# Layer 0 of a two-layer fp32 kernel: the front's bank in a new order, delta's replicas behind its store, 1+e on GpSimd

## The chip, the cores and the metric

The program runs on one core of a Trainium2 chip, in one launch. The metric is the device time of the whole program in microseconds. The engines are PE (TensorE), DVE (VectorE), ACT (ScalarE), POOL (GpSimd) and SP (SyncE, which issues nearly all DMAs here). Each engine works through its own list of instructions in order and waits on semaphores; nothing is reordered while it runs.

## What is computed

Two layers, each a sequence mixer and an expert layer added to the residual. The change touches layer 0 alone, on 8192 tokens of width 128:

```
xn    = layernorm(x)
u, z  = split(rmsnorm(xn) @ in_proj)            # 256 + 256 channels
xi    = silu(conv4(u) + conv_b)
dt, B, C = split(xi @ x_proj)                   # 8, 16, 16
delta = softplus(dt @ dt_w + dt_b)
h     = exp(delta * A) * h + (delta * xi) * B   # a scan over time, 16 states a channel
y     = (sum over states of h * C + xi * D) * silu(z)
p     = softmax(xn @ Wr + br); gate = p where the sorted cumulative sum < 0.8, else 0
ffn   = sum over 8 experts of gate_e * (relu(xn @ W1_e + b1_e) @ W2_e + b2_e)
x     = x + (xn + y @ out_proj) + ffn
```

## The kernel before

Layer 0 goes through the tokens in 16 iterations of 512 tokens. In an iteration the scan has 32 tiles of 128 x 512 (two halves of the channels, four groups of states, four channel blocks), and each of the 8 experts has four `up` products into two banks (`UP`) and a `down` product into `DN`.

The order of the work is written out by hand. An iteration is 32 half-slots h = 0..31, and every engine runs through the same h in its own list:

- DVE: `scan(h)`, then `times_c(h)` (the product with C). The scan needs `dA` (h) and `dBx`.
- ACT: `make_da(h + 2)`, exp(delta * A), into a ring of three PSUM banks; for h mod 4 = 0 and 1 also two `relu`, one before and one after it; for h mod 4 = 3 the gate times the expert's output.
- POOL: at even h `make_dbx`, the products delta * x * B for half-slots h + 2 and h + 3; at h mod 4 = 2 one `accumulate`.
- PE: `up` products at h mod 4 = 0 and 1, the sum over states (`add_states`, bank `YS`) at h mod 4 = 1, one half of a `down` product at 2 and at 3. An `up` of one group of four half-slots is used by the `down` of the next group.

Between these, each engine makes the *front* of the next iteration: norm, transposes, in_proj, convolution, x_proj, delta, logits, gate and silu(z). The front's TensorE products share one PSUM bank, `FRO`, so they follow each other as the bank is emptied. The tables `PE_AT`, `ACT_AT`, `DVE_AT`, `POOL_AT` and `SP_AT` give for each piece the half-slot after whose own work it is put into the engine's list; a negative number counts back from the end of the iteration before. Pieces of one engine with the same h stand in the order of the code of `fore`.

Softplus is made as max(v,0) + log(1+e) with e = exp(-|v|), v = dt @ dt_w + dt_b, and with a correction of what is lost in 1+e: `one_w` = 1+e; `soft` = (one_w - 1) - e (DVE); `umax` = umax - soft ("r", POOL); ln(1+e) (ACT, which loads another table for it and the first again after it); `lnw`, that logarithm where 1+e is over 1 (DVE); delta = umax + lnw (POOL); dx = delta * xi (POOL). The gate's first steps are the logits, their maximum (DVE "lg"), the difference (POOL "lg"), and the exponential (ACT "gexp").

delta, dx, B and C go to HBM and come back as replicas over the partitions (`REP`: 1 MB for each of delta and dx and each half, `BC`: 1 MB for each two groups of states). SP issues these stores and loads, in its own order.

Of the kernel before, what the change touches and what calls it, by code (L numbers as in the profile page):

```python
# [51 lines left out]
def layer0(nc, ctx, t, dram, scratch):  # L52
# [35 lines left out]
    forget = sb("forget", [P, T0 // L]); mean = sb("mean", [P, NT]); rstd = sb("rstd", [P, NT]); rrms = sb("rrms", [P, NT])  # L88
# [26 lines left out]
    front = signal("front", 11)  # L115
# [4 lines left out]
    sp_done = signal("sp_done", 3); relu_done = signal("relu_done", E0 * FB); da_ready = signal("da_ready", TILES); gated = signal("gated", E0)  # L120
# [134 lines left out]
    def _(sp):  # L255
# [68 lines left out]
        def fore(h, n, q):  # L324
# [47 lines left out]
    def _(pe):  # L372
        for s in (front, upf, downf, sumf, outf):
            pe.sem_inc(s.sem, 2 * s.per)
# [71 lines left out]
        def slot(h, it, par, first=False, final=False, last_front=False):  # L446
# [13 lines left out]
            if h == PE_AT["out"] and not first:  # L460
                if final:
                    output(it - 1, 1 - par, lambda: pe.wait_ge(gT_copied.sem, gT_copied.at(it, 1)))
                else:
                    output(it - 1, 1 - par, lambda: pe.wait_ge(conv_step.sem, conv_step.at(it + 1, 6)))

        def fore(h, n, q):
            if h == PE_AT["xqt"]:
# [46 lines left out]
            for k in range(HALF):  # L514
                if h == PE_AT[f"z{k}"]:

                    if k == 0:
                        pe.wait_ge(gate_step.sem, gate_step.at(n, 1))
                    elif bank(n, k) is FRO:
                        pe.wait_ge(z_done.sem, z_done.at(n, 1))  # L520
                    nc.tensor.matmul(bank(n, k)[:], inproj[:, (2 + k) * P:(3 + k) * P], xrT[:], start=True, stop=True).then_inc(front.sem, 1)
            if h == PE_AT["gt"]:

                pe.wait_ge(gate_made.sem, gate_made.at(n, 5))
                pe.wait_ge(z_done.sem, z_done.at(n, 2))
                nc.tensor.transpose(FRO[0:J0 * E0, 0:P], gate[:, q].rearrange("p j e -> p (j e)"), ident[:]).then_inc(front.sem, 1)
# [13 lines left out]
    def _(act):  # L540
# [103 lines left out]
        def fore(h, n, q):  # L644
# [50 lines left out]
            for k in range(HALF):  # L695
                if h == ACT_AT[f"tz{k}"]:

                    if k == 0:
                        act.wait_ge(delta_done.sem, delta_done.at(n, 1))
# [1206 lines left out]
```

## Time and profile before

| what | value |
|---|---|
| median of three runs | 2101.07 us (2100.62 to 2101.74) |
| the profiled execution | 2100.98 us, its span 2099.2 us |
| around the span | 1.78 us |
| PE busy | 1894.3 us, 90% |
| DVE busy | 1675.4 us, 80% |
| ACT busy | 1341.5 us, 64% |
| POOL busy | 1309.0 us, 62% |
| first scan of layer 0 / last statistics of layer 0 | 74.3 us / 1426.8 us |

The span is the time from the first to the last instruction of the profiled execution; its own time is longer by what lies around the span. Busy is the time in which an engine ran an instruction. Layer 0's sixteen iterations lie between the first scan and the last statistics; the rest belongs to the start and to layer 1.

### The profile page before, as it was taken

The numbers are of one execution on the slowest core, as the hardware profiler recorded it, in microseconds if no ns is written. First come the engines' busy times: TensorE is split into PE (matmuls) and PEld (weight loads), VectorE is DVE, ScalarE is ACT, GpSimd is POOL, SyncE is SP. The second block draws the span as 40 slices with busy tenths as digits, with TensorE's granted clock in tenths as the row PEclk, the third lists the DMA queues.
The fourth block names the chain that finished last, engine by engine and source line by source line (L and its number), as shares of the span: only waits on it lengthen the run. The fifth ranks groups of instructions, "written<-read, shape, count | busy, mean of one in ns | idle before, by whom it ended". The sixth has DMA issues, their size and how long they took to land. (4 is left out here: it accounts for less than half of the span.)

```text
span 2099.2 us, 39052 instructions
## 1 busy us (share of the span) xinstructions
PE 1894.3 (90%) x14321; PEld 1106.2 (53%) x14321; DVE 1675.4 (80%) x2731; ACT 1341.5 (64%) x2423; POOL 1309.0 (62%) x1005
## 2 busy tenths in 40 slices
PE   5789999999999999999999999994799999998985
PEld 3445555555555555555555555552455555554552
DVE  5588888898898987988979888883888888886655
ACT  3577776776777767777677677761355555554652
POOL 2577877868878777787786887863343333333650
PEclk7899999999999999999999999996799999999997
DMA  8633615426245163362451633605444444455558
GB/s 202 155 85 73 141 40 125 101 52 141 75 90 133 30 140 87 67 141 58 106 120 43 136 87 68 141 6 156 123 119 123 117 117 117 117 137 154 163 145 245
DMA packets 211994, 234.86 MB, mean 112 GB/s; under 512 B 31718, under 2 KB 150414, under 8 KB 207694
## 3 DMA queue, kind: packets, MB, share of 16 engines
q1 hardware_dynamic: 207116, 227.95, 43.7%
q0 software_dynamic: 2048, 4.18, 0.7%
q8 instruction: 115, 1.88, 0.4%
q14 instruction: 75, 0.61, 0.1%
q10 hardware_dynamic: 2640, 0.24, 0.1%
HBM read 165.48 MB, written 66.85 MB: 111 GB/s over the span
## 5 line engine op out<-in xcount | busy, mean ns | idle before, releaser
L731 POOL TENSOR_TENSOR dBx<-REP,BC 128x1024 f32<-128x1024 f32 x256 | 603.6, 2360 | 254.7 <-DVE dA L904 224.6
L904 DVE TENSOR_TENSOR_SCAN dA<-dA,dBx 128x512 f32<-128x512 f32 x512 | 626.3, 1223 | 154.4 <-POOL dBx L731 109.9
L403 PE MATMUL UP<-xnT,W 128*128 128x512 f32 x1024 | 517.6, 623 | 49.3 <-ACT hT L605 44.6
L412 PEld LDWEIGHTS DN<-W,hT 128*128 128x128 f32 x4096 | 469.5, 192 | 98.0 <-issue 66.9
L412 PE MATMUL DN<-W,hT 128*128 128x128 f32 x4096 | 495.1, 278 | 0.3 <-ACT GD L612 0.3
L596 ACT ACTIVATE dA<-REP,A 128x512 f32<-128x512 f32 x512 | 354.0, 695 | 86.5 <-DVE PR L913 78.0
L605 ACT ACTIVATE hT<-UP,b 128x512 f32<-128x512 f32 x512 | 355.6, 695 | 66.1 <-PE UP L403 60.6
L913 DVE TENSOR_TENSOR PR<-dA,BC 128x512 f32<-128x512 f32 x512 | 353.6, 691 | 16.0
L403 PEld LDWEIGHTS UP<-xnT,W 128*128 128x128 f32 x1024 | 179.1, 194 | 286.9 <-issue 163.7
L1808 DVE TENSOR_REDUCE NM<-S 128x4 f32<-128x1024 f32 (+1 forms) x192 | 234.1, 1219 | 76.0 <-PE S L1353 75.8
L1567 ACT ACTIVATE PT<-S 128x1024 f32<-128x1024 f32 x192 | 197.1, 1027 | 94.8 <-PE S L1353 94.0
L612 ACT ACTIVATE GD<-DN,gate 128x128 f32<-128x128 f32 x512 | 145.6, 366 | 126.6 <-PE DN L412 126.1
L741 POOL TENSOR_TENSOR FF<-FF,GD 128x512 f32<-128x512 f32 x128 | 162.8, 1272 | 6.1 <-ACT GD L612 6.1
L424 PE MATMUL YS<-PR,fold 128*32 128x512 f32 x1024 | 139.7, 618 | 0.5 <-DVE PR L913 0.5
L1621 POOL TENSOR_TENSOR t<-t 128x512 f32<-128x512 f32 x32 | 40.7, 1271 | 133.4 <-DVE t L1732 133.3
L1409 PE MATMUL OT<-PT,V 128*9 128x256 f32 x1024 | 84.7, 392 | 7.2 <-ACT PT L1567 5.2
L1548 ACT CAST CS<-ACC 128x256 bf16<-128x256 f32 x64 | 23.8, 373 | 84.9 <-PE ACC L1465 83.7
L1627 POOL TENSOR_TENSOR SPL<-t,SPL 128x512 bf16<-128x512 f32 x32 | 37.2, 1162 | 65.6 <-ACT SPL L1573 65.6
L970 DVE SCALAR_TENSOR_TENSOR xch<-FRO,convw,xch 128x510 f32<-128x510 f32 (+2 forms) x93 | 69.2, 744 | 8.6 <-ACT xch L655 6.4
L1561 ACT COPY OSB<-OT 128x512 f32<-128x512 f32 x64 | 37.5, 586 | 59.2 <-PE OT L1411 59.2
L424 PEld LDWEIGHTS YS<-PR,fold 128*32 128x32 f32 x1024 | 20.4, 109 | 102.8 <-issue 68.1
L797 POOL TENSOR_TENSOR xch<-xch,soft 128x1024 f32<-128x1024 f32 x16 | 37.6, 2350 | 43.3 <-DVE soft L979 43.3
(251 smaller groups left out, 2618.1 us busy)
## 6 DMA issues: line engine op xcount, KB each, us to landing
BC<-s_b SPq DMA_DIRECT2D x128, 256.0 KB, 5.9
REP<-s_dx SPq DMA_DIRECT2D x124, 256.0 KB, 7.5
REP<-s_delta SPq DMA_DIRECT2D x124, 256.0 KB, 8.9
s_parts<-SPL SPq DMA_DIRECT2D x64, 192.0 KB
KS<-s_parts SPq DMA_DIRECT2D x64, 192.0 KB
QS<-s_parts SPq DMA_DIRECT2D x64, 192.0 KB
s_dx<-tz SPq DMA_DIRECT2D x16, 512.0 KB, 3.1
s_y<-zeros SPq DMA_DIRECT2D x32, 256.0 KB, 2.9
```

Of the source, the lines that this page charges most:

```text
L403: nc.tensor.matmul(UP[k % 2][:], W1[:, e % E0, f * P:(f + 1) * P], xnT[:, q, :], start=True, stop=True).then_inc(upf.sem, 1)
L412: last = nc.tensor.matmul(DN[:, j * P:(j + 1) * P], hT[:, e % 2, f, j * P:(j + 1) * P], W2[:, e, f, :], start=(f == 0), stop=(f == FB - 1))
L424: last = nc.tensor.matmul(YS[CB * j:CB * j + CB, :], fold[:], PR[:, (DB * b + j) % (2 * DB), :], start=(q == 0), stop=(q == NQ - 1), tile_ ...
L596: nc.scalar.activation(dA[:, k % 3, :], DR[:, h, j, :], ACT.Exp, scale=A[:, h, j, q:q + 1]).then_inc(da_ready.sem, 1)
L605: nc.scalar.activation(hT[:, e % 2, f, :], UP[k % 2][:], ACT.Relu, bias=b1[:, e % E0, f:f + 1]).then_inc(relu_done.sem, 1)
L612: last = nc.scalar.activation(GD[:, e % 2, j, :], DN[:, j * P:(j + 1) * P], ACT.Copy, scale=gate[:, par, j, e:e + 1])
L731: nc.gpsimd.tensor_tensor(dBx[:, s % 2], DX[:, h, j:j + 2, :], BC[:, q // 2, q % 2, :].unsqueeze(1).to_broadcast([P, 2, T0]), ALU.mult).th ...
L741: nc.gpsimd.tensor_tensor(FF[:, par], FF[:, par], GD[:, e % 2], ALU.add).then_inc(acc_done.sem, 1)
L904: nc.vector.tensor_tensor_scan(h, h, dBx[:, k // 2 % 2, k % 2, :], 0.0, ALU.mult, ALU.add).then_inc(scan_done.sem, 1)
L913: nc.vector.tensor_tensor(PR[:, k % (2 * DB), :], dA[:, k % 3, :], BC[:, q // 2, 2 + q % 2, :], ALU.mult).then_inc(prod_done.sem, 1)
L1567: nc.scalar.activation(PT[:, u // 3, u % 3, :], S2[:].rearrange("p b w -> p (b w)"), ACT.Exp, scale=SCALE).then_inc(exp_done.sem, 1)
L1808: nc.vector.tensor_reduce(NM[:, 0 if a == 0 else 1, :].rearrange("p (r i) -> p r i", r=2)[:, :, heads], S1[:].rearrange("p r (j k) -> p r ...
```

## The change

Four things are changed, all in layer 0.

1. The front's bank goes in another order. The first transpose (`xqt`) moves from h = -2 to -6, the two products of u (`x0`, `x1`) and their convolutions four half-slots earlier, `xnt` from 17 to 4, x_proj from 10 to 8, `dt0` and `dt1` from 12 and 16 to 10 and 14, `z1` now stands ahead of `z0` (20 and 23, were 27 and 23), and the transpose of the gate goes from the front into the next iteration (h = 16). POOL's norm of the tokens (`xm`, `xq`, `xs`) moves from -7, -4, -4 to -19, -17, -15, and `EARLY` from 7 to 19 so that this can be written.
2. `one_w` = 1+e is an addition on POOL (h = 15) in place of an ACT instruction (h = 17), with a tile `unit` of ones broadcast as second operand; the correction is written to `one_w` and not over `soft`, and the test for a lost e reads e itself. ACT's exp goes from 17 to 14.
3. On POOL `r` goes from 20 to 18 and `dx` from 23 to 21, where it stands ahead of `lg`.
4. On SP the loads of delta's first replicas follow its store directly, and those of dx stand behind the loads of B and C.

```diff
-    umax, lnw, one_w, tanhz = xch, th, tz, xch
+    umax, lnw, one_w = xch, th, tz
...
-    EARLY = 7
-    PE_AT = dict(xqt=-2, x0=0, x1=4, out=8, xproj=10, dt0=12, dt1=16, xnt=17, logits=19, z0=23, z1=27, gt=29)
-    ACT_AT = dict(xr=-2, tap0=2, tap1=4, tanh=6, dtb=10, d0=14, d1=16, xn=18, exp=17, one=17, ln=18, gexp=20, tz0=23, tz1=27, gt=29)
-    DVE_AT = dict(conv0=3, conv1=5, xi=8, soft=19, lg=19, lnw=20, gate1=23, z0=25, gate2=27, z1=29, ev1=3, store=9, stat=12, ev0=21)
-    POOL_AT = dict(xm=-7, xq=-4, xs=-4, ff=10, r=20, dx=23, rank=23, yz1=3, yz0=22, delta=20, lg=21, keep=27)
+    EARLY = 19
+    PE_AT = dict(xqt=-6, x0=-4, x1=0, xnt=4, out=6, xproj=8, dt0=10, dt1=14, gt=16, logits=18, z1=20, z0=23)
+    ACT_AT = dict(xr=-6, tap0=-2, tap1=0, tanh=2, xn=5, dtb=9, d0=10, d1=14, exp=14, gt=17, ln=18, gexp=20, tz1=21, tz0=25)
+    DVE_AT = dict(conv0=-1, conv1=1, xi=4, soft=17, lg=19, lnw=20, gate1=23, z1=23, z0=25, gate2=27, ev1=3, store=7, stat=11, ev0=21)
+    POOL_AT = dict(xm=-19, xq=-17, xs=-15, ff=9, one=15, r=18, dx=21, rank=23, yz1=3, yz0=22, delta=20, lg=21, keep=27)
...
-    SP_AT = dict(bst=11, dst=15, est=23, bc0=26, save=10, load=12)
+    SP_AT = dict(bst=9, dst=15, est=23, bc0=26, save=8, load=10)
...
+                if not start:
+                    load_delta(0, n, q)
             elif h == SP_AT["est"]:
...
-                else:
-                    load_delta(0, n, q)
-                    load_dx(0, n, q)
             elif h == SP_AT["bc0"] and not start:
                 load_states(0, n, q)
+                load_dx(0, n, q)
...
+            if h == PE_AT["z1"]:
+
+                pe.wait_ge(gate_step.sem, gate_step.at(n, 1))
+                nc.tensor.matmul(bank(n, 1)[:], inproj[:, 3 * P:4 * P], xrT[:], start=True, stop=True).then_inc(front.sem, 1)
+            if h == PE_AT["z0"]:
+
+                if bank(n, 1) is FRO:
+                    pe.wait_ge(z_done.sem, z_done.at(n, 1))
+                nc.tensor.matmul(FRO[:], inproj[:, 2 * P:3 * P], xrT[:], start=True, stop=True).then_inc(front.sem, 1)
...
-            if h == ACT_AT["one"]:
-                act.wait_ge(sp_done.sem, sp_done.at(n, 1))
-                act.wait_ge(e_stored.sem, e_stored.at(n - 1, 16))
-                nc.scalar.activation(one_w[:], soft[:], ACT.Identity, bias=1.0).then_inc(sp_done.sem, 1)
...
+            if h == POOL_AT["one"]:
+
+                pool.wait_ge(sp_done.sem, sp_done.at(n, 1))
+                pool.wait_ge(e_stored.sem, e_stored.at(n - 1, 16))
+                nc.gpsimd.tensor_tensor(one_w[:], soft[:], unit[:].unsqueeze(1).to_broadcast([P, HALF, T0]), ALU.add).then_inc(one_done.sem, 1)
             if h == POOL_AT["r"]:
...
+            if h == POOL_AT["dx"]:
+
+                pool.wait_ge(delta_done.sem, delta_done.at(n, 1))
+                nc.gpsimd.tensor_tensor(dx[:], delta[:], xi[:, q], ALU.mult).then_inc(dx_done.sem, 1)
             if h == POOL_AT["lg"]:
                 pool.wait_ge(gate_step.sem, gate_step.at(n, 2))
                 nc.gpsimd.tensor_tensor(lg[:], lg[:], g4[:, 0, :].unsqueeze(2).to_broadcast([P, J0, E0]), ALU.subtract).then_inc(lg_done.sem, 1)
-            if h == POOL_AT["dx"]:
...
-                dve.wait_ge(sp_done.sem, sp_done.at(n, 2))
-                nc.vector.scalar_tensor_tensor(soft[:], one_w[:], -1.0, soft[:], ALU.add, ALU.subtract).then_inc(log_step.sem, 1)
+                dve.wait_ge(one_done.sem, one_done.at(n, 1))
+                nc.vector.scalar_tensor_tensor(one_w[:], one_w[:], -1.0, soft[:], ALU.add, ALU.subtract).then_inc(log_step.sem, 1)
...
-                nc.vector.scalar_tensor_tensor(lnw[:], one_w[:], 1.0, lnw[:], ALU.is_gt, ALU.mult).then_inc(log_step.sem, 1)
+                nc.vector.scalar_tensor_tensor(lnw[:], soft[:], LOST, lnw[:], ALU.is_gt, ALU.mult).then_inc(log_step.sem, 1)
...
+            if h == DVE_AT["z1"]:
+
+                dve.wait_ge(tanh_z.sem, tanh_z.at(n, 1))
+                dve.wait_ge(yz_done.sem, yz_done.at(n - 2, 2))
+                nc.vector.scalar_tensor_tensor(z1[:, q, :], tanhz[:], 1.0, bank(n, 1)[:], ALU.add, ALU.mult).then_inc(z_done.sem, 1)
```

## Rows read from the trace of the kernel before

**Rows 1.** Windows: stretch, length, busy PE, PEld, DVE, ACT, POOL, PE clock, DMA.

```profile
707.13:733.82 26.69, 24.01 (x149) 15.73 (x146) 23.08 (x28) 22.41 (x41) 19.34 (x11) 1.00 0.06 20
733.82:791.70 57.88, 56.21 (x292) 31.25 (x290) 49.53 (x62) 39.10 (x76) 46.35 (x34) 1.00 0.58 129
701.08:785.65 84.57, 80.22 (x437) 46.97 (x437) 72.60 (x89) 61.51 (x115) 65.68 (x45) 1.00 0.41 95
```

**Rows 2.** Waits in 701.08:785.65: who waited for whom, total, times, longest.

```profile
DVE dA L904 <- POOL dBx L731: 6.6, 2, 5.0
...
ACT pe_ L694 <- POOL lg L804: 0.5, 1, 0.5
```

**Rows 3.** Timeline of PE: start, length, instruction.

```profile
707.13 3.84 PE L412 MATMUL DN<-W,hT 128*128 128x128 f32 x32
...
712.62 1.12 PE L500 MATMUL FRO<-dtB,dtw 8*128 8x512 f32 x2
...
732.96 1.02 PE L521 MATMUL FRO<-xrT,inproj 128*128 128x512 f32 x2
```

**Rows 4.** Timeline of ACT; in brackets the idle time before.

```profile
713.78 0.72 ACT L641 ACTIVATE xch<-FRO,dtb 128x512 f32<-128x512 f32 x1
...
716.69 1.10 ACT L682 ACTIVATE soft<-soft 128x1024 f32<-128x1024 f32 x1
717.82 1.06 ACT L686 ACTIVATE tz<-soft 128x1024 f32<-128x1024 f32 x1
...
727.71 0.23 ACT L694 ACTIVATE pe_<-lg 128x32 f32<-128x32 f32 x1 [0.53 <-POOL lg L804]
727.85 0.67 ACT L605 ACTIVATE hT<-UP,b 128x512 f32<-128x512 f32 x1
728.42 0.68 ACT L596 ACTIVATE dA<-REP,A 128x512 f32<-128x512 f32 x1
```

**Rows 5.** Timeline of POOL, the same columns.

```profile
717.58 2.36 POOL L731 TENSOR_TENSOR dBx<-REP,BC 128x1024 f32<-128x1024 f32 x1 [2.28 <-DVE dA L904]
721.11 2.35 POOL L797 TENSOR_TENSOR xch<-xch,soft 128x1024 f32<-128x1024 f32 x1 [1.16 <-DVE soft L979]
...
727.45 0.23 POOL L804 TENSOR_TENSOR lg<-lg,g 128x32 f32<-128x32 f32 x1
727.64 2.37 POOL L731 TENSOR_TENSOR dBx<-REP,BC 128x1024 f32<-128x1024 f32 x1
729.97 1.27 POOL L741 TENSOR_TENSOR FF<-FF,GD 128x512 f32<-128x512 f32 x1
731.20 1.27 POOL L747 TENSOR_TENSOR y<-y,z 128x512 f32<-128x512 f32 x1
...
740.60 1.04 POOL L780 TENSOR_TENSOR XN<-XI,mean 128x512 f32<-128x512 f32 x1
```

**Rows 6.** Timeline of DVE, the same columns.

```profile
718.91 2.12 DVE L979 SCALAR_TENSOR_TENSOR soft<-tz,soft 128x1024 f32<-128x1024 f32 x1 [0.68 <-ACT tz L686]
...
729.21 1.22 DVE L904 TENSOR_TENSOR_SCAN dA<-dA,dBx 128x512 f32<-128x512 f32 x1
...
731.07 0.17 DVE L993 TENSOR_REDUCE g<-pe_ 128x4 f32<-128x32 f32 x1
...
731.37 1.22 DVE L904 TENSOR_TENSOR_SCAN dA<-dA,dBx 128x512 f32<-128x512 f32 x1
...
735.09 0.68 DVE L999 SCALAR_TENSOR_TENSOR z<-xch,FRO 128x512 f32<-128x512 f32 x1
```

**Rows 7.** Single lines: count, shortest, median and longest ns, first and last start.

```profile
L979 DVE SCALAR_TENSOR_TENSOR soft<-tz,soft x16: 1226/2117/2870, 42.4 to 1312.2; 128x1024 f32<-128x1024 f32 x16
...
L731 POOL TENSOR_TENSOR dBx<-REP,BC x256: 2342/2360/2391, 71.8 to 1408.5; 128x1024 f32<-128x1024 f32 x128
```

**Rows 8.** Timeline of SP's DMA queue, the replicas and B, C.

```profile
735.29 2.31 SPq L264 DMA_DIRECT2D REP<-s_delta  x4
...
740.01 14.98 SPq L269 DMA_DIRECT2D BC<-s_b  x8
```

More of the change, by code:

```diff
@@ L38 @@
 FORGET, SLOWEST = 1e20, -1e-17
+LOST = 2.0 ** -24
 class Signal:
@@ L112, in layer0 @@
     FRO = ctx.enter_context(nc.psum_tensor("FRO", [P, 512], F32))
-    front = signal("front", 11)
+    front = signal("front", 10); turned = signal("turned", 1)
     upf = signal("upf", E0 * FB); downf = signal("downf", E0); sumf = signal("sumf", HALF * NQ); outf = signal("outf", 1)
@@ L372, in _ @@
     def _(pe):
-        for s in (front, upf, downf, sumf, outf):
+        for s in (front, turned, upf, downf, sumf, outf):
             pe.sem_inc(s.sem, 2 * s.per)
@@ L461, in slot @@
                 if final:
-                    output(it - 1, 1 - par, lambda: pe.wait_ge(gT_copied.sem, gT_copied.at(it, 1)))
+                    output(it - 1, 1 - par, lambda: pe.wait_ge(z_done.sem, z_done.at(it, 2)))
                 else:
-                    output(it - 1, 1 - par, lambda: pe.wait_ge(conv_step.sem, conv_step.at(it + 1, 6)))
+                    output(it - 1, 1 - par, lambda: pe.wait_ge(xT_copied.sem, xT_copied.at(it + 1, 2)))
+            if h == PE_AT["gt"]:
+                pe.wait_ge(gate_made.sem, gate_made.at(it, 5))
+                if final:
+                    pe.wait_ge(x_done.sem, x_done.at(it - 1, 1))
+                else:
+                    pe.wait_ge(u_done.sem, u_done.at(it + 1, 2))
+                nc.tensor.transpose(FRO[0:J0 * E0, 0:P], gate[:, par].rearrange("p j e -> p (j e)"), ident[:]).then_inc(turned.sem, 1)
         def fore(h, n, q):
@@ L513, in fore @@
                 last.then_inc(front.sem, 1)
[L514 to L526, printed above, removed]
+            if h == PE_AT["z1"]:
[5 more added lines that the diff above has]
+                nc.tensor.matmul(FRO[:], inproj[:, 2 * P:3 * P], xrT[:], start=True, stop=True).then_inc(front.sem, 1)
         def between(s):
@@ L634, in slot @@
                 apply_gate(s // 2, it, par)
+            if h == ACT_AT["gt"]:
+                act.wait_ge(outf.sem, outf.at(it - 2, 1))
+                act.wait_ge(turned.sem, turned.at(it, 1))
+                nc.scalar.copy(gT[:, par, :], FRO[0:J0 * E0, 0:P]).then_inc(gT_copied.sem, 1)
             if first and h in ROOTS_AT:
@@ L638, in delta_input @@
         def delta_input(k, n):
-            act.wait_ge(front.sem, front.at(n, 5 + k))
+            act.wait_ge(front.sem, front.at(n, 6 + k))
             nc.scalar.activation(umax[:, k, :], bank(n, k)[:], ACT.Relu, bias=dtb[:, k:k + 1])
@@ L661, in fore @@
             if h == ACT_AT["dtb"]:
-                act.wait_ge(front.sem, front.at(n, 4))
+                act.wait_ge(front.sem, front.at(n, 5))
                 act.wait_ge(b_stored.sem, b_stored.at(n - 1, 16))
@@ L676, in fore @@
                 act.wait_ge(upf.sem, upf.at(n - 2, E0 * FB))
-                act.wait_ge(front.sem, front.at(n, 7))
+                act.wait_ge(front.sem, front.at(n, 4))
                 nc.scalar.copy(xnT[:, q, :], FRO[:]).then_inc(xT_copied.sem, 1)
@@ L682, in fore @@
                 nc.scalar.activation(soft[:], soft[:], ACT.Exp, scale=-1.0).then_inc(sp_done.sem, 1)
-            if h == ACT_AT["one"]:
+            if h == ACT_AT["ln"]:
                 act.wait_ge(sp_done.sem, sp_done.at(n, 1))
-                act.wait_ge(e_stored.sem, e_stored.at(n - 1, 16))
-                nc.scalar.activation(one_w[:], soft[:], ACT.Identity, bias=1.0).then_inc(sp_done.sem, 1)
-            if h == ACT_AT["ln"]:
-                act.wait_ge(sp_done.sem, sp_done.at(n, 2))
-                nc.scalar.activation(lnw[:], one_w[:], ACT.Ln).then_inc(sp_done.sem, 1)
+                nc.scalar.activation(lnw[:], soft[:], ACT.Ln, bias=1.0).then_inc(sp_done.sem, 1)
             if h == ACT_AT["gexp"]:
@@ L696, in fore @@
                 if h == ACT_AT[f"tz{k}"]:
[L698 to L705 removed]
+                    act.wait_ge(z_done.sem, z_done.at(n, 0 if k else 1))
+                    act.wait_ge(front.sem, front.at(n, 10 - k))
+                    nc.scalar.activation(tanhz[:], bank(n, k)[:], ACT.Tanh, scale=0.5).then_inc(tanh_z.sem, 1)
         pipeline(fore, start, slot, lambda it, par: None, act, between)
@@ L710, in _ @@
     def _(pool):
-        for s in (xn_ready, dbx_ready, yz_done, acc_done, delta_done, dx_done, lg_done, rank_step, gate_made, r_done):
+        for s in (xn_ready, dbx_ready, yz_done, acc_done, delta_done, dx_done, lg_done, rank_step, gate_made, r_done, one_done):
             pool.sem_inc(s.sem, 2 * s.per)
@@ L774, in fore @@
                     pool.wait_ge(stat_step2, 21)
-                pool.wait_ge(front.sem, front.at(n - 1, 7))
+                pool.wait_ge(front.sem, front.at(n - 1, 4))
                 pool.wait_ge(xi_loaded.sem, xi_loaded.at(n, 16))
```

46 lines of the change are left out of this document (18 added, 28 removed).

## The prediction

> **What bounds the kernel now.** I read the windows first: an iteration of layer 0 lasts 84.57 us, from one group of statistics to the next. PE is busy for 80.22 us of it, DVE for 72.60, POOL for 65.68, ACT for 61.51, with TensorE at its full clock (2.4 GHz, granted 1.00) [rows 1]. So PE is the bound, and what this change can give back is at most PE's idle time: 4.35 us an iteration. Split at half-slot 14 and 24 (PE's `down` at 707.13 and its `up` behind `z0` at 733.82), 2.68 us of it lie in the first, short stretch and 1.67 us in the other [rows 1].
>
> The waits then say why PE runs dry: around h = 26 DVE waited once 5.0 us for POOL's `dBx`, while ACT's gate exponential waited only 0.5 us for POOL's `lg` [rows 2]. These are the two places to follow. The timelines show the order there: POOL does `r`, then delta, then `lg` at 727.45, and dx only after the next `dBx`; gexp runs at 727.71, and right behind it in ACT's list come a `relu` and the `dA` of h = 23 [rows 4, 5]. ACT's list is in order, so **whatever delays POOL's `lg` delays `dA`, the scan, and all that DVE does behind it.** That is where I think the change is decided.
>
> **The change part by part**, counted from the start of PE's `down` half at h = 14 (707.13 in [rows 3]), which in the new kernel is still set by PE alone.
>
> *Work taken off.* ACT loses one instruction of 1.06 us [rows 4]; ACT has 23 us of idle time in an iteration and is not the bound, so by itself this is worth nothing but a shorter block of ACT. PE, DVE and the matmuls keep their counts.
>
> *The chain up to exp.* Half a `down` takes about 1.9 us (3.84 for the whole), `dt1` 1.12 [rows 3], d1's two ACT instructions 1.3 (0.72 each, issued 0.57 apart as the pair at 727.85), exp 1.10 [rows 4]: exp ends at 5.5, and POOL's `one` starts at 5.6. POOL's list has nothing it could do meanwhile: the next `xq`, `dBx` and `xs` stand behind `one`.
>
> *POOL from `one` to `lg`.* `one` itself no row shows. From below, a broadcast operand on 512 columns took 1.04, so 2.08 for 1024; from above, two full operands of the same width took 2.35 (721.11) [rows 5]. I take 2.2; the difference is 0.3 us. Then follow, each by its distance to the next start, `xq` 1.0, `dBx` 2.33, `xs` 1.0, `dBx` 2.33, `accumulate` 1.23, `r` 2.33, `dBx` 2.33, delta 2.33, dx 2.33, `lg` 0.2 (same rows; r, delta and dx have the shape of 721.11). The sum is 19.6, so `lg` ends at 25.25. No wait in between is longer: the third `dBx` of the chain ends at 20.4, and `lnw`, which delta needs, at about 18.2 (the first `dBx` of the chain at 11.15, two slots of 1.86 and a tenth or two of `lg`, another slot, 1.1 for `lnw`).
>
> *From `lg` to the next group.* gexp 0.14 to the next start, `relu` 0.57, `dA` 0.71 to the scan [rows 4]; a slot of DVE is 1.86 (729.21 to 731.07), the gate's two small steps 0.30, `z1` 0.68 [rows 6]. With `z1` ahead of `z0`, PE's `z0` at h = 23 waits for exactly this `z1`, then takes 0.86 (732.96 to 733.82) [rows 1, 3]; a hand-off is 0.15. Sum: 25.3 + 1.42 + 1.86 + 0.30 + 0.68 + 0.15 + 0.86 = 30.6 us. **Before, the same stretch took 26.69 [rows 1], so it is 3.9 longer.** PE, which has work for some 24 us there, stands for over 5 us at `z0`.
>
> *The port that DVE and POOL share.* The correction `soft` lasts 1.23 us at its shortest and 2.87 at its longest [rows 7]. At 718.91 it lasted until 1.09 us after POOL's `dBx` (717.58 + 2.36) had ended [rows 5, 6]: it stood still while POOL worked, then ran its 1.1 us. Before, `r` waits for `soft` and delta for `lnw`, so POOL then idled. Now POOL has work behind work, and `soft` and `lnw`, both with two operands in SBUF, fall into it. Does POOL wait for them in turn? No row shows it: all 256 `dBx` last 2.34 to 2.39 [rows 7]. From below it costs the chain nothing; if each of the two gets in after the instruction that POOL is in, 1.1 us each, 2.2 in all; from above, if POOL goes on until it needs `soft` itself, `soft` comes after `accumulate`, at 15.7, and the chain is 3.7 longer (1.1 for `soft`, 1.1 for the slots behind it, 1.5 until `lnw`). The row at 718.91 is an exclusive turn, not a sharing, so I take 2.2: the stretch lasts 32.8, which is 6.1 more than before.
>
> The Trainium skill's page SBUF — State Buffer ("SBUF: two separate sides") states it as a rule: a DVE instruction with two SBUF inputs and a GpSimd instruction that reads SBUF exclude each other for a whole instruction, and the one that starts first blocks the other. The trace agrees for the half that it shows, DVE behind POOL (2.12 in place of 1.23 us). By the rule POOL is blocked as well, which is the 6.1; without it the sum would be the 3.9.
>
> *What the other stretch gets back (57.88 before).* Its idle time, 1.67, bounds the gain from below [rows 1]. The 5.0 us wait of DVE [rows 2] goes, as dx no longer stands between `dBx` and the ranks. Of PE's work `z1` and the gate's transpose leave it and `xnt` comes in: 0.5 less. Against it, `x1` right behind `conv0` waits about half a microsecond. Both ways it is 1.7 to 2.4; I take 2.0.
>
> *DMA.* SP issued delta's replicas at 735.29, and B and C behind dx from 740.01 on, drawn out to 755.0 [rows 8]. Now delta's 1 MB is issued behind delta's store, while POOL still makes dx, and B and C go ahead of dx. ACT needs delta's replicas and POOL those of dx only at h = 30; by the sum above dx is ready before h = 23, so some seven half-slots, 13 us at 1.86 or more, cover the loads. I cost the new order at nothing; without that cover the stretch of [rows 8], up to 15 us, would lie open in each iteration.
>
> **The sum.** Per iteration +6.1 - 2.0 = +4.1 us. The front is made inside the loop 15 times: 61 us, less than 1 us more at the start (`one` is 1.1 slower, once). 2100.98 is the profiled execution's time, 0.1 under the median of the runs: **2162 us, 2.9% slower.**
>
> **The rivals.**
> 1. *The order is right but POOL isn't held up* by `soft` and `lnw`: +3.9 - 2.0 = +1.9, 15 times: 2129 us. For it: no stretched POOL row. Against it: the exclusive turn of DVE. With the upper bound of the port, +3.9 + 3.7 - 2.0 = +5.6: 2185 us.
> 2. *POOL's backlog doesn't form* (this one ends on the other side). If `dBx` of h = 22 ended at 18.2, when `lnw` does, and not at 20.4, `lg` would end at 23.1 and the stretch at 28.4; +1.7 - 2.0 = -0.3: 2096 us. It takes POOL 2.2 us less between exp and delta. If the wait for `lg` went altogether, DVE would reach `z1` at 25.3 and PE the end at 26.3: -0.4 - 2.0, 2065 us. It decides from where `lg` ends under 23.4. For it: POOL has 19 us idle in an iteration [rows 1]. Against it: the list is in order, the idle time lies before exp, not after it, and each term from exp to `lg` is a row.
> 3. *The change makes no difference*, since PE is the bound in both: the stall at `z0` would just equal the two stalls before. About 2097 to 2105.
>
> **How the numbers follow.** My forecast, with POOL held up by one or both or the upper bound, 0.55; rival 1 without any hold-up 0.25; rival 2 0.13; rival 3 0.07. A measurement of this kernel tells about 0.2% (4 us) from no change. So slower 0.80, same 0.07, faster 0.13. The range goes from 2106 (a little under rival 1, whose `one`, hand-offs and gain are each known to some tenths; below it lie rivals 2 and 3) to 2186, the upper bound of the port.
>
> **What the profile after would show.** Right: ACT's gexp waits 6 to 10 us for POOL's `lg`, where it was 0.5; PE's `z0` waits about 5 us or more for DVE's `z1`; POOL has hardly a gap from `one` to `lg`; the 5.0 us wait of a scan for `dBx` near h = 26 is gone; `soft` lasts about 2 us, and a start of POOL comes 1.1 us after `soft` began its own part. An iteration lasts some 88.7 us. Wrong: gexp waits under 4 us, or exp comes earlier than 5.5 us after PE's half-slot 14 because PE is no longer what sets it; then the front's new order wins and the kernel is faster.

## The result and the profile after

The changed kernel takes 2230.41 us, the median of four runs (2226.45 to 2232.41), beside 2101.40 for the kernel before: 6.1% slower, ratio 1.0613 with a 95% interval of 1.059 to 1.0635. The direction was forecast, the size not: 129 us were lost in place of 61, and the time lies outside the range. The profiled execution has a span of 2230.6 us (before 2099.2). An iteration takes 92.03 us and no longer 84.57 [rows 1]; the first scan starts at 92.0 us, where it was 74.3.

The windows of one iteration after, split as in [rows 1] at PE's half-slot 14 and behind `z0`, then the whole iteration, then four short pieces around the end of `z0` (columns as there):

```profile
684.99:718.08 33.09, 25.81 (x148) 16.42 (x145) 22.98 (x29) 20.58 (x39) 27.29 (x17) 0.94 0.19 46
718.08:777.02 58.94, 57.43 (x294) 31.90 (x292) 51.02 (x61) 40.07 (x76) 42.11 (x29) 0.97 0.50 110
700.91:792.94 92.03, 83.24 (x436) 48.32 (x435) 74.00 (x89) 60.65 (x115) 69.39 (x46) 0.96 0.38 87
712.00:714.00 2.00, 0.00 (x0) 0.00 (x0) 0.70 (x1) 2.00 (x5) 2.00 (x1) 1.00 0.24 29
714.00:716.00 2.00, 0.00 (x0) 0.00 (x0) 1.93 (x5) 2.00 (x6) 2.00 (x3) 0.55 0.98 241
...
718.00:720.00 2.00, 2.00 (x4) 0.89 (x3) 1.85 (x3) 0.00 (x0) 1.72 (x3) 0.50 1.06 328
...
722.00:724.00 2.00, 2.00 (x11) 0.45 (x10) 0.00 (x0) 1.83 (x4) 2.00 (x2) 1.00 1.04 227
```

The first stretch, up to the end of `z0`, lasts 33.09 us (forecast 32.8, before 26.69). The other lasts 58.94 (forecast 57.88 - 2.0 = 55.9). So nearly the whole miss inside the loop lies in the other stretch, and its PE is busier than before (57.43 against 56.21), not idler. The short pieces show one reason: PE stood, and the granted clock fell from 1.00 to 0.50, the 1.2 GHz level, and was 1.00 again only in the last piece.

The chain in the timelines of POOL, ACT, DVE and PE (it answers to [rows 3 to 6]):

```profile
690.55 1.89 POOL L800 TENSOR_TENSOR tz<-soft,unit 128x1024 f32<-128x1024 f32 x1 [5.62 <-ACT soft L692]
692.40 1.04 POOL L786 TENSOR_TENSOR XQ<-XN,q 128x512 f32<-128x512 f32 x1
693.40 3.35 POOL L733 TENSOR_TENSOR dBx<-REP,BC 128x1024 f32<-128x1024 f32 x1
...
703.57 3.33 POOL L733 TENSOR_TENSOR dBx<-REP,BC 128x1024 f32<-128x1024 f32 x1
706.86 2.36 POOL L808 TENSOR_TENSOR soft<-xch,th 128x1024 f32<-128x1024 f32 x1
709.30 2.35 POOL L812 TENSOR_TENSOR tz<-soft,xi 128x1024 f32<-128x1024 f32 x1
711.61 0.24 POOL L815 TENSOR_TENSOR lg<-lg,g 128x32 f32<-128x32 f32 x1
...
711.88 0.23 ACT L700 ACTIVATE pe_<-lg 128x32 f32<-128x32 f32 x1 [8.17 <-POOL lg L815]
...
692.96 1.56 DVE L986 SCALAR_TENSOR_TENSOR tz<-tz,soft 128x1024 f32<-128x1024 f32 x1
...
702.78 1.92 DVE L996 SCALAR_TENSOR_TENSOR th<-soft,th 128x1024 f32<-128x1024 f32 x1
...
713.30 1.23 DVE L911 TENSOR_TENSOR_SCAN dA<-dA,dBx 128x512 f32<-128x512 f32 x1 [4.34 <-ACT dA L602]
...
715.49 0.67 DVE L1006 SCALAR_TENSOR_TENSOR z<-tanhz,FRO 128x512 f32<-128x512 f32 x1
...
724.73 0.69 DVE L1011 SCALAR_TENSOR_TENSOR z<-tanhz,FRO 128x512 f32<-128x512 f32 x1 [4.84 <-ACT tanhz L706]
...
707.61 3.84 PE L413 MATMUL DN<-W,hT 128*128 128x128 f32 x32
716.21 2.08 PE L532 MATMUL FRO<-xrT,inproj 128*128 128x512 f32 x2 [4.76 <-DVE z L1006]
718.08 5.26 PE L404 MATMUL UP<-xnT,W 128*128 128x512 f32 x8
```

POOL goes without a gap from 1+e at 690.55 to `lg` at 711.61; ACT's gexp stands 8.17 us for `lg`, the scan 4.34 for ACT's `dA`, PE's `z0` 4.76 for `z1`. Two of the `dBx` last 3.35 and 3.33 us, where all 256 of before lay between 2.34 and 2.39 [rows 7]: they overlap the correction `soft` (692.96) and `lnw` (702.78) on DVE. Behind the wait, `z0` and the `up` products run at half clock (2.08 and 5.26 us; the same eight `up` products take 4.11 at full clock, in the iteration of e1 shown below). And DVE then stands 4.84 us for ACT's tanh of `z0`, a wait that my prediction doesn't have.

The waits of the iteration 700.91 to 792.94 (who waited for whom, total, times, longest), against [rows 2]:

```profile
ACT pe_ L700 <- POOL lg L815: 8.2, 1, 8.2
...
PE FRO L532 <- DVE z L1006: 4.8, 1, 4.8
...
DVE dA L911 <- POOL dBx L733: 2.8, 2, 2.3
```

The scan's 5.0 us wait for `dBx` is gone, gexp's 0.5 has become 8.2. Last, the start: POOL, and SP's queue.

```profile
58.31 1.04 POOL L782 TENSOR_TENSOR XN<-XI,mean 128x512 f32<-128x512 f32 x1 [40.38 <-DMA XI<-in_L_attn_x]
59.30 1.89 POOL L800 TENSOR_TENSOR tz<-soft,unit 128x1024 f32<-128x1024 f32 x1
...
42.06 10.90 SPq L344 DMA_DIRECT2D b<-in_L_ffn_b  x4
...
53.63 0.39 SPq L313 DMA_DIRECT2D XI<-in_L_attn_x  x1
```

With `xm` at h = -19, the norm of block 1 stands in POOL's list ahead of block 0's 1+e. Its tokens are loaded behind the weights in SP's list, at 53.63, so POOL stood 40.38 us, and block 0's delta with it.

### The profile page after: what moved, and what is told of

Its sections match the earlier page's. It is cut to its first block and busy times, and to the rows that moved or that the text cites. A ratio compares the mean times of both kernels' runs of the same rounds, so it can differ in the third digit from the quotient of the medians.

```text
span 2230.6 us, 39088 instructions
## 1 busy us (share of the span) xinstructions
PE 1929.1 (86%) x14321; PEld 1121.3 (50%) x14321; DVE 1699.9 (76%) x2731; ACT 1323.8 (59%) x2407; POOL 1366.9 (61%) x1022
## 5 line engine op out<-in xcount | busy, mean ns | idle before, releaser
L733 POOL TENSOR_TENSOR dBx<-REP,BC 128x1024 f32<-128x1024 f32 x256 | 630.9, 2470 | 162.7 <-DVE dA L911 156.9
L404 PE MATMUL UP<-xnT,W 128*128 128x512 f32 x1024 | 532.3, 637 | 30.5 <-ACT hT L611 26.3
L413 PE MATMUL DN<-W,hT 128*128 128x128 f32 x4096 | 507.5, 279 | 0.3 <-ACT GD L618 0.3
L404 PEld LDWEIGHTS UP<-xnT,W 128*128 128x128 f32 x1024 | 186.6, 201 | 282.5 <-ACT hT L611 151.4
L532 PE MATMUL FRO<-xrT,inproj 128*128 128x512 f32 x32 | 32.8, 1129 | 69.4 <-DVE z L1006 69.4
L800 POOL TENSOR_TENSOR tz<-soft,unit 128x1024 f32<-128x1024 f32 x16 | 30.3, 1892 | 82.0 <-ACT soft L692 82.0
```

Source lines behind the costliest of these rows:

```text
L404: nc.tensor.matmul(UP[k % 2][:], W1[:, e % E0, f * P:(f + 1) * P], xnT[:, q, :], start=True, stop=True).then_inc(upf.sem, 1)
L413: last = nc.tensor.matmul(DN[:, j * P:(j + 1) * P], hT[:, e % 2, f, j * P:(j + 1) * P], W2[:, e, f, :], start=(f == 0), stop=(f == FB - 1))
L733: nc.gpsimd.tensor_tensor(dBx[:, s % 2], DX[:, h, j:j + 2, :], BC[:, q // 2, q % 2, :].unsqueeze(1).to_broadcast([P, 2, T0]), ALU.mult).th ...
```

## The experiments

My first theory after the result had three parts: **P**, POOL's longer chain to `lg` (with 1+e, the blocked `dBx` and dx in it) makes `z0` wait, and the wait costs the clock too; **S**, the start; **B**, the new order itself costs, wherever 1+e is made. The rivals were that one of them carries all of the loss, and that the new order is a gain which only 1+e on POOL hides. A fourth part, **T**, the place of the tanh of `z0`, came up when e1 had been read. "Iteration" below is the mean of ten iterations in the middle of layer 0: 84.71 us before, 92.18 after. Where nothing else is said, the edit is made to the changed kernel.

The expectations, written ahead of each run, use other letters: P is "theory A" there (and "C" where POOL's backlog alone is meant), S is "theory P", and B is "theory B". Two parts of the change that its list doesn't name also bear on the runs. ACT's logarithm is taken of e with a bias of 1, so it no longer waits for 1+e, even where 1+e is back on ACT. And the tanh of z has a tile of its own. Both stay in all runs made from the changed kernel, and the first is in e8 too.

**e1: `lg` ahead of dx on POOL.**

```diff
+            if h == POOL_AT["lg"]:
...
             if h == POOL_AT["dx"]:
...
-            if h == POOL_AT["lg"]:
```

> Theory A (the gate exponential on ACT stands behind POOL's lg, and lg behind the whole POOL chain from 1+e to dx; PE's z0 waits for what follows, and TensorE's clock is at half for some 5 us after that stall): with lg ahead of dx, lg ends 2.3 us earlier, so z0's wait falls from 4.8 to about 2.4 us in each of 15 iterations, and if the clock then stays at full another 2.5 us come back: 36 to 74 us off the 2230, so 2156 to 2194. Theory B (the stretch is longer because the front's shared bank is refilled in a worse order, lg's place does not matter): within 5 us of 2230.

**e2: block 1's norm where it was.**

```diff
-            if h == POOL_AT["xm"]:
+            late = isinstance(n, int) and n == 1
+            if h == (-7 if late else POOL_AT["xm"]):
...
-            if h == POOL_AT["xq"]:
+            if h == (-4 if late else POOL_AT["xq"]):
...
-            if h == POOL_AT["xs"]:
+            if h == (-4 if late else POOL_AT["xs"]):
```

> Theory P (before the first scan, POOL's list holds the norm of the second block ahead of 1+e, and it waits 40 us for a load that SP issued behind all the weights): with the three norm instructions of block 1 alone put behind dx, where they stood before, the first scan starts at 74 to 76 us and not at 92.0, the loop stays at 92.0 us an iteration: about 2212. Rival: the first scan is late because the first loads of replicas are later in SP's queue; then nothing moves.

**e3: 1+e back on ACT**, at h = 14 behind exp.

```diff
-            if h == POOL_AT["one"]:
...
+            if h == 14:
...
+                nc.scalar.activation(one_w[:], soft[:], ACT.Identity, bias=1.0).then_inc(one_done.sem, 1)
```

> 1+e back on ACT, right behind exp, the rest as in the changed kernel. Theory A: POOL no longer stands still until exp is done, and 1.9 us of its chain are gone, so lg ends some 4 to 4.5 us earlier, z0 hardly waits, the clock stays at full: 7 us an iteration, 105 us in all, near 2122 (the late start stays). Theory B: only ACT's 1.06 us and POOL's 1.9 us change, off the bound: 2220 to 2235.

**e4: the gate's exponential later**, so that `z0` needs no `lg`.

```diff
-    gexp=20    gate1=23, gate2=27    rank=23, keep=27
+    gexp=22    gate1=24, gate2=29    rank=24, keep=30
```

> POOL's work and its order untouched but for the ranks; only ACT's gate exponential goes from h = 20 to 22, behind tanh of z1, and what hangs on it one to three half-slots later. Theory A: dA of h = 23 and z1 no longer wait for lg; z0's wait falls under 1 us, the clock stays at full; POOL's late dBx then shows instead, some 1 to 3 us an iteration on DVE. About 6 to 7.5 us an iteration: 2118 to 2140. If POOL's backlog itself is what costs (rival C), DVE waits for dBx about as long as it waited for dA and the time stays over 2190.

| run | median, us | ratio to before (95%) | iteration, us | first scan, us |
|---|---|---|---|---|
| the change | 2230.41 | 1.0613 (1.0590 to 1.0635) | 92.18 | 92.0 |
| e1 | 2187.01 | 1.0389 (1.0360 to 1.0419) | 89.18 | 94.5 |
| e2 | 2215.65 | 1.0528 (1.0499 to 1.0558) | 92.18 | 78.7 |
| e3 | 2178.54 | 1.0344 (1.0305 to 1.0382) | 88.80 | 88.3 |
| e4 | 2167.24 | 1.0289 (1.0256 to 1.0322) | 87.92 | 92.3 |

e2 settles most of the start: the iteration is untouched, the first scan 13.3 us earlier, and POOL's 1+e of block 0 begins at 42.01 and not at 59.30. e1, e3 and e4 each take 3.0 to 4.3 us off an iteration by shortening or removing the same wait, but none comes near 84.71. e3 and e4 end between what their two theories gave, so P is a part of the loss and not the whole. `z0` and the `up` products behind it, in PE's timelines of e1, then e3, then e4, where the last two lines are `x1` and its `up`:

```profile
697.31 1.12 PE L532 MATMUL FRO<-xrT,inproj 128*128 128x512 f32 x2 [2.34 <-DVE z L1006]
698.28 4.11 PE L404 MATMUL UP<-xnT,W 128*128 128x512 f32 x8
```

```profile
688.71 1.41 PE L532 MATMUL FRO<-xrT,inproj 128*128 128x512 f32 x2 [2.54 <-DVE z L1006]
689.92 5.24 PE L404 MATMUL UP<-xnT,W 128*128 128x512 f32 x8
```

```profile
684.47 1.12 PE L532 MATMUL FRO<-xrT,inproj 128*128 128x512 f32 x2
...
708.39 1.12 PE L491 MATMUL FRO<-xrT,inproj 128*128 128x512 f32 x2 [2.69 <-DVE xch L977]
709.35 3.40 PE L404 MATMUL UP<-xnT,W 128*128 128x512 f32 x4
```

In this iteration of e1 the wait is 2.34 us and the clock stays full, yet the stretch behind `z0` lasts 59.39 us, as its window shows, no less than the 58.94 of the changed kernel. Two whole iterations of e1 follow it, from `z0` to `z0`, one with the clock fallen behind the same wait and one with it full:

```profile
698.28:757.67 59.39, 56.70 (x294) 31.11 (x292) 52.50 (x63) 40.03 (x76) 45.15 (x33) 1.00 0.55 121
...
251.26:340.43 89.17, 82.47 (x435) 47.97 (x436) 74.17 (x88) 60.65 (x115) 69.37 (x46) 0.98 0.40 90
697.31:786.45 89.14, 81.61 (x435) 47.18 (x435) 74.18 (x88) 60.60 (x115) 69.33 (x46) 1.00 0.40 90
```

The clock fell in nine of fourteen such iterations of e1 and changed nothing in their length. So in e1 the half clock isn't what that stretch lost: DVE waits there, 2.12 us for the tanh of `z0` and then 1.67 for `dBx`. In e3 the wait is 2.54 and the `up` products run at half clock again. In e4 `z0` stands directly behind its `down` without a wait; but now `x1` waits 2.69 us for the first convolution, and the clock falls there (0.50 in 710 to 712 us). The stall is moved, not gone.

**e5: e1, e2 and e4 together**, and **e6: those and 1+e on ACT** (e3's edit too).

> Three of the edits together: lg ahead of dx, block 1's norm behind dx at the start, gexp at h = 22. If the edits on gexp only share one stall (both take away the same wait), the time is the one with gexp late less the start's 15 us, 2140 to 2155. If they add up, 2105 to 2125. Theory C (what is left is POOL's backlog: scans wait for dBx, the convolution comes late, x1 on PE waits for it): scans still wait 80 to 110 us for dBx and PE 30 to 50 us at x1.

> The kernel before this with 1+e back on ACT as well. Theory C: POOL's chain loses 1.9 us and its standstill until exp, the waits of scans for dBx and of x1 for the convolution nearly go: 4 to 6 us an iteration less than the kernel with the three edits, 2060 to 2090, faster than before the change. Rival (the order of the bank leaves PE's x1 and xnt waiting whatever POOL does): under 2 us an iteration less.

e5: 2156.10 us, 1.0256 (1.0238 to 1.0274), iteration 87.81, which is e4's: with gexp late, the place of `lg` is worth nothing. e6: 2114.52 us, 1.0069 (1.0053 to 1.0085), iteration 85.33, less gained than the 4 to 6 us expected. So 1+e on ACT is worth 2.5 us an iteration even where `z0` doesn't wait, and what is left of the change is, in this form, still no gain.

**e8: the kernel before with 1+e on POOL alone** (h = 18).

```diff
-            if h == ACT_AT["one"]:
...
+            if h == POOL_AT["one"]:
...
+                nc.gpsimd.tensor_tensor(one_w[:], soft[:], unit[:].unsqueeze(1).to_broadcast([P, HALF, T0]), ALU.add).then_inc(one_done.sem, 1)
```

> The kernel before the change, with 1+e on POOL (h = 18, behind accumulate) and the correction written over it, and nothing else moved. If 1+e on GpSimd is itself a loss: POOL's dBx and r come 1.9 us later, 1 to 2 us an iteration, 2115 to 2130. If its cost is the place that it has in the changed kernel: POOL waited for exp here anyway, ACT's block before PE's relu is 1 us shorter, 2085 to 2105.

**e9: the bank's order alone**: e2 and e3, and the rest of POOL's list and SP's order as before.

```diff
-    r=18, dx=21
+    r=20, dx=23
...
-                if not start:
-                    load_delta(0, n, q)
             elif h == SP_AT["est"]:
...
+                else:
+                    load_delta(0, n, q)
+                    load_dx(0, n, q)
             elif h == SP_AT["bc0"] and not start:
                 load_states(0, n, q)
-                load_dx(0, n, q)
```

> The bank's new order with POOL's early norm and exp at h = 14, but 1+e on ACT, r at 20 and dx at 23 behind lg, SP's old order of loads, block 1's norm behind dx at the start. Theory A and C: nothing of POOL's stands between exp and lg any more, z0 and gexp hardly wait; PE is the bound: 2 to 4 us an iteration under the kernel before, 2040 to 2075. Theory B (the bank's order is the loss): 2110 or more.

e8: 2136.00 us, 1.0169 (1.0153 to 1.0186), iteration 86.82. 1+e on POOL loses 2.1 us an iteration without any of the rest, a little more than the 1 to 2 expected of a loss. e9: 2159.86 us, 1.0288 (1.0271 to 1.0305), iteration 88.38. The order with 1+e on ACT loses 3.7, so part B holds. PE's `up` at half-slot 17 waited 1.94 us for a `relu` there, and POOL 3.9 on the mean for B and C. That gave two candidates for B, which the next four runs separate.

**e10: e9 with the new order of loads. e11: e10 with exp and 1+e at ACT's h = 17, `soft` at DVE's 19. e12: e11 with the gate later, as e4. e13: the kernel before with the new order of loads alone.**

```diff
 e11
-    exp=14    soft=17
+    exp=17    soft=19
-            if h == 14:
+            if h == 17:
```

```diff
 e13
+                if not start:
+                    load_delta(0, n, q)
             elif h == SP_AT["est"]:
...
-                else:
-                    load_delta(0, n, q)
-                    load_dx(0, n, q)
             elif h == SP_AT["bc0"] and not start:
                 load_states(0, n, q)
+                load_dx(0, n, q)
```

> The changed kernel with 1+e back on ACT (h = 14, behind exp), POOL's `lg` ahead of dx, `r` and dx at 20 and 23 as before, block 1's norm in its old place, and the loads in the CHANGED order: it differs from the run with the bank's order alone (88.72 us an iteration, 2159.9) in the loads' order only. Theory D (in the new bank order the old load order costs, because POOL waited 4.2 us an iteration for B and C): 86 to 87.5 us an iteration, 2120 to 2142. Theory H (ACT's block of d1, exp and 1+e at h = 14 costs, the loads' order nothing): 88.7 again, 2155 to 2163.

> As the run before it, with exp and 1+e at ACT's h = 17 and the correction `soft` at DVE's h = 19, their places before the change; d1 stays at 14. What is left of the change is the bank's order, the gate's transpose in the next iteration and the order of loads. Theory H (the block of d1, exp and 1+e at h = 14 holds up ACT's `relu` and `dA`, and PE's `up` behind it by 1.9 us): at least 1.9 us an iteration less than the run before it. Theory B (the bank's order costs wherever exp stands, through x1, xnt and their copies): within 1 us of the run before it. Under 84.6 us an iteration and 2101 us the bank's order would be a gain by itself.

> As the run before it, with the gate's exponential and what follows it later (ACT gexp 22, DVE gate1 24, gate2 29, POOL rank 24, keep 30), which lets PE's z0 go without waiting for POOL's `lg`. If z0 still waits for `lg` in the run before it: 1 to 2.5 us an iteration less, 2080 to 2115. If the stalls only move to the scans, as they did when the gate alone was put later in the changed kernel: within 0.5 us an iteration of the run before it.

> The kernel BEFORE with only the order of loads changed: delta's replicas issued behind delta's store, those of dx behind the loads of B and C. The prediction's term (hidden, nothing): 2097 to 2105. Rival (B and C landing earlier takes away the scan's 5.0 us wait for `dBx`, which had waited for them): 0.5 to 2 us an iteration less, 2070 to 2093. Rival (dx's replicas come too late and POOL's first `dBx` of the next iteration waits): 1 us an iteration more or worse, over 2116.

| run | median, us | ratio to before (95%) | iteration, us |
|---|---|---|---|
| e10 | 2155.46 | 1.0268 (1.0254 to 1.0283) | 88.17 |
| e11 | 2109.03 | 1.0039 (1.0026 to 1.0052) | 85.04 |
| e12 | 2087.99 | 0.9946 (0.9931 to 0.9961) | 83.66 |
| e13 | 2092.00 | 0.9962 (0.9949 to 0.9975) | 84.02 |

Theory D falls: beside e9, the order of loads is worth 0.2 us an iteration. Theory H holds: exp and 1+e three half-slots later give 3.1 us, with DVE's `soft` two later in the same edit, whose share wasn't tried alone. The place, in the timelines of ACT and PE, first of e10:

```profile
736.98 0.69 ACT L651 ACTIVATE xch<-FRO,dtb 128x512 f32<-128x512 f32 x1 [2.76 <-PE FRO L509]
...
738.28 1.06 ACT L692 ACTIVATE soft<-soft 128x1024 f32<-128x1024 f32 x1
739.37 1.06 ACT L697 ACTIVATE tz<-soft 128x1024 f32<-128x1024 f32 x1
740.33 0.67 ACT L602 ACTIVATE dA<-REP,A 128x512 f32<-128x512 f32 x1
...
742.69 3.26 PE L404 MATMUL UP<-xnT,W 128*128 128x512 f32 x4 [1.94 <-ACT hT L611]
```

and of e11:

```profile
714.58 0.68 ACT L652 ACTIVATE soft<-FRO,dtb 128x512 f32<-128x512 f32 x1
715.15 0.69 ACT L602 ACTIVATE dA<-REP,A 128x512 f32<-128x512 f32 x1
...
717.75 2.31 PE L404 MATMUL UP<-xnT,W 128*128 128x512 f32 x4
```

In e10 ACT has already stood 2.76 us at d1 for `dt1`; exp and 1+e behind it put the next `dA` and `relu` off by about 2.1 us more, PE waits 1.94 us, and its four `up` products take 3.26 us, most of it at half clock. DVE's scan waits 4.15 us for that `dA`, and 1.97 in e11. The clock isn't what costs here: it fell in seven of thirteen such iterations, and all are 88.15 to 88.20 us long. In e11 `dA` follows d1 at once and PE doesn't wait there: PE is busy 81.32 us of 85.03 at clock 1.00.

What e12 gains over e11 isn't what its expectation names. `z0` had no wait in e11. `x1` had, as the timelines of PE show (e11, then e12):

```profile
758.92 1.12 PE L491 MATMUL FRO<-xrT,inproj 128*128 128x512 f32 x2 [1.43 <-DVE xch L978]
```

```profile
748.65 1.12 PE L491 MATMUL FRO<-xrT,inproj 128*128 128x512 f32 x2
```

and with the gate later the convolution ahead of it is reached in time. e12 beats the kernel before by 0.5%, with the new bank order and loads, but without 1+e on POOL, exp at 14, and `lg` behind dx.

**e14 to e16: the tanh of `z0` back to ACT's h = 23** in the changed kernel, in e11 and in e12. **e17: that tanh alone at 25 in the kernel before.** The change had put it from 23 to 25, and so behind the four `relu` of the next group.

```diff
 e14, e15, e16
-    tz0=25
+    tz0=23
 e17
-    tz0=23
+    tz0=25
```

> The changed kernel with ACT's tanh of z0 at h = 23 (its place before the change) and not at 25. Theory T (DVE's wait of 4.8 us for this tanh holds up the scans and the convolution behind it, and so PE's x1): the wait is gone and the stretch behind z0 falls by 1.5 to 3 us, 89.2 to 90.7 us an iteration in place of 92.2, 2185 to 2208. Rival C (the half clock behind the stall at z0, or POOL, sets that stretch): less than 0.5 us an iteration, 2223 or more.

> The kernel with the new bank order and loads, 1+e on ACT, exp at 17 (85.04 us an iteration, 2109) with ACT's tanh of z0 at 23. Theory T: DVE's wait of 3.5 us goes, and with it the 1.43 us that x1 waits for the first convolution: 83.4 to 84.2 an iteration, 2083 to 2097. Rival G (x1 waits because the gate's steps stand ahead of the convolution, and only the later gate helps): within 0.4 us of 85.04.

> The fastest version so far (new bank order and loads, 1+e on ACT, exp at 17, gate later; 83.66 an iteration, 2088) with ACT's tanh of z0 at 23. Theory T, where x1 has no wait left to lose: 0 to 1 us less an iteration, 2072 to 2089. Rival (ACT, waiting at the tanh for PE's z0, holds up the `dA` of the next half-slots): slower, over 2093.

> The kernel BEFORE with only ACT's tanh of z0 moved from 23 to 25. Theory T: DVE waits 3 us or more for it in each iteration, and since DVE waited 5.0 us for `dBx` right behind z0 there, part of that is hidden: 0 to 2 us an iteration more, 2101 to 2132. Rival (hidden wholly by that wait): 2097 to 2105.

| run | median, us | ratio to before (95%) | iteration, us |
|---|---|---|---|
| e14 | 2194.00 | 1.0453 (1.0437 to 1.0469) | 89.86 |
| e15 | 2107.96 | 1.0036 (1.0022 to 1.0049) | 85.01 |
| e16 | 2081.25 | 0.9917 (0.9904 to 0.9931) | 83.08 |
| e17 | 2101.47 | 1.0006 (0.9997 to 1.0015) | 84.69 |

e14 shows T in the changed kernel: 2.3 us an iteration, 36 us in all. `z0`'s own wait is as before it, so the first stretch stays; the other one shrinks. Windows of e14, the two stretches of an iteration and then the other stretch of the next two:

```profile
670.33:703.42 33.09, 25.82 (x147) 16.42 (x144) 22.97 (x29) 20.57 (x39) 27.28 (x17) 0.95 0.16 41
703.42:760.71 57.29, 57.14 (x293) 32.09 (x291) 51.31 (x61) 39.89 (x76) 42.12 (x29) 0.97 0.52 116
...
793.26:850.12 56.86, 56.71 (x293) 31.82 (x291) 51.52 (x62) 40.00 (x76) 42.59 (x29) 0.98 0.53 117
...
883.21:939.81 56.60, 56.39 (x293) 31.61 (x291) 51.10 (x61) 39.82 (x76) 42.12 (x29) 0.99 0.51 115
```

PE is now idle for 0.15 to 0.21 us of the other stretch, which lasts 56.92 on the mean of the three. From their start to the next, the eight `up` products behind `z0` take 5.46, 5.03 and 4.76 us in these three, where they take 4.04 at full clock. Without that surplus the stretches last 55.87, 55.87 and 55.88 us: here, with PE hardly idle, the half clock adds its whole length.

In e15 the tanh is worth nothing: DVE's wait goes, but `x1` still waits 1.42 us, so the gate's steps ahead of the convolution set it (rival G). In e16, where those are out of the way, it gives 0.6 us an iteration, and e16 is the fastest version, 0.8% under the kernel before. In e17 DVE waits 4.4 us an iteration for the tanh (69.7 in 16) and the time doesn't change: there the scan behind it would have waited for `dBx` anyway [rows 2]. The sums over the whole run, before and then e17 (DVE's waits for the tanh and for `dBx`), show it: what the one gains the other loses.

```profile
DVE z L999 <- ACT xch L701: 10.0, 10, 2.0
...
DVE dA L904 <- POOL dBx L731: 109.9, 32, 17.3
```

```profile
DVE z L999 <- ACT xch L701: 69.7, 16, 5.6
...
DVE dA L904 <- POOL dBx L731: 50.0, 25, 17.2
```

## Why the prediction was wrong

*What decides.* Right in the chain: POOL's `lg` holds up gexp, `dA`, the scan and `z1`, and PE stands at `z0`. Each wait named in advance is in the profile at about its size (8.17 for "6 to 10", 4.76 for "about 5").

"So PE is the bound" isn't borne out for the kernel before. Of thirteen iterations five, that of [rows 1] among them, ran at a clock of 1.00. In the other eight the clock fell behind a stall of 2.6 us at `up`, PE was busy 1.2 to 1.5 us longer, and the iterations were as long, 84.8 us on the mean against 84.7. The one that follows [rows 1]:

```profile
785.65:870.48 84.83, 81.45 (x437) 47.44 (x437) 72.80 (x89) 61.96 (x115) 65.66 (x45) 0.98 0.41 94
```

There PE's idle time takes up what the clock costs, so PE's work alone doesn't set the length.

*The first stretch.* Right in size, 33.09 for 32.8, with two errors that cancel. `lg` ended 26.86 us after half-slot 14 (forecast 27.45), since 1+e took 1.89 us, under the bound of 2.08 that I drew from a row of half its width, and the two blocked `dBx` cost 0.99 and 0.97 and not 1.1 each. `z0` then took 1.87 us to the next start and not 0.86, at half clock.

*The port.* Right, against rival 1. `soft` began at 692.96, while `XQ` was under way (until 693.44), and lasted 1.56 in place of 1.23 (about 2 was forecast); the `dBx` begun at 693.40 was then 0.99 longer than usual. Each stood for the other in turn. The Trainium skill's page SBUF — State Buffer ("SBUF: two separate sides") says that whichever starts first holds the shared pair for its whole instruction; the trace agrees, for POOL as well as DVE.

*"The other stretch gets back 2.0 us": the step that failed.* It lost 1.06 (58.94 for 57.88), a miss of 3.06. Some 1.9 of it is the tanh of `z0`, which I didn't follow when it went from 23 to 25. With the tanh at 25 DVE's wait for `dBx`, which did go, comes back as one for ACT; back at 23, in e14, PE's idle time, 1.67 us before, is gone nearly whole, as the step said. The remaining 1.15 are the half clock: the eight `up` products behind `z0` take 5.19 us to the next start and not 4.04. I had priced a stall at its own length only. Without both the stretch would last the 55.9 us of the forecast, as e14's three do without the surplus of their `up` products.

*"Less than 1 us more at the start."* It was 17.7 us later at the first scan. I followed the delay of 1+e itself but not what the change puts ahead of it: `xm` at -19 stands before block 0's 1+e in POOL's list, and its load behind the weights in SP's. e2 shows 13.3 us of it on the first scan and 14.8 on the whole. The other 4.4 weren't separated; 1+e on POOL alone (e8) puts the first scan 1.6 us later than before, the order with 1+e on ACT (e11) 2.8.

*The whole.* From the first scan to that of the sixteenth iteration, fifteen iterations took 1380.4 us, and 1274.1 before: 106 us more and not 61, a little under fifteen times the one shown, since the first and the last lost less. With 17.7 at the start that is 124 of the 131 us between the two profiled spans. The other 7 lie behind: 2.6 in the last iteration's scans, and the rest where hardly anything was changed and where the profiles of all these runs lie up to 8 us apart.

*"ACT loses one instruction, by itself nothing; exp ends at 5.5."* Both figures hold, but I didn't ask what the earlier exp does to ACT's own list. Exp with 1+e at h = 14, and `soft` at 17, cost 3.1 us an iteration (e10 against e11), for the most part by `dA` and `relu` behind them. In the changed kernel itself 1+e isn't on ACT there, so how much exp alone loses at 14 was not tried.

*The order of loads, at nothing.* Too low by a little: alone it gains 0.7 us an iteration (e13, 8.8 us in all). In the kernel before, B and C were issued over 14.98 us from 740.01 on [rows 8]; in e13 their first half is issued at 728.44, ahead of dx's replicas. In the new bank order the same edit gives 0.2.

*The rivals.* Rival 2 needed `lg` to end under 23.4: it ended at 26.86, but e16 (83.08 us an iteration) shows that the order can win, with 1+e, exp, `lg` and the tanh at their old places and the gate later; the order of loads alone, e13, has 84.02. Rival 3's wait, equal to those before, didn't come about either. No case had a tanh that comes late, a clock that falls or a late start, and the range's upper bound summed the port alone.

## What to carry to other kernels

When a table of places changes, go through every entry that moved, the ones that look like a detail too, and write down what now stands ahead of each in its engine's list, the first iteration included: two entries that I passed over, the tanh of `z0` and the norm of block 1, cost 36 and 15 us. Where PE has hardly any idle time, price a new stall at its length and at what the work behind it takes at half clock (up to 1.4 us in e14); where another engine sets the stretch, as in e1, that second part cost nothing. And price an instruction that goes to another engine by what its new neighbours then wait: the 1.89 us of 1+e on POOL cost 2.1 to 3.4 us an iteration (e8, e6, e3).

## What the runs showed of the hardware

The granted clock fell after short stalls. In the changed kernel it was 0.50, the 1.2 GHz level, when PE went on at 716.21 after it had stood 4.76 us, and 1.00 again in 722 to 724. The length of a stall doesn't decide it alone: in e1 fourteen stalls of 2.33 or 2.34 us at `z0` left the clock at 1.00 five times, and it fell nine times; in e3 it fell behind all of fourteen, those of 1.93 us as well as those of 2.54; in the kernel before, behind nine of fourteen stalls of 2.62 us at `up`. The Trainium skill's page TensorE: Matmul & The Clock Gate ("Part 1: The HAM clock gate") says that activity releases the throttle and idleness brings back the half rate; the rows agree.

An addition on POOL with a second operand broadcast along the row took 1.89 us for 128 x 1024, less than twice the 1.04 of the 128 x 512 subtraction in [rows 5], and less than the 2.36 of two full operands. A POOL instruction of 2.36 us became 3.35 when a two-operand instruction of DVE got in ahead of it.
